# Linear attention behind a sparse feed-forward layer: gathers issued right behind GpSimd's buffer sums, and the query mean placed later in a batch's first tile

## The reference

```
xn  = layernorm(x)
out = x + attention(xn) + ffn(xn)

attention: q, k, v = xn @ w.T, 16 heads of 16; sq = elu(q) + 1; sk = elu(k) + 1
  memory: a_m = sq @ M_m, n_m = sq . z_m           (4 fine memories, and their sum as the coarse one)
          rel_m = mean over the 1024 tokens of n_m  -> w = softmax over the 4 memories
          out_fine = sum_m w_m * a_m / n_m ;  out_coarse = a / n
          e = sigmoid(relu(out_coarse @ w1 + b1) @ w2 + b2); mix of fine and coarse by e
  local : causal linear attention in chunks (scores = sq sk^T * mask, plus the carried state)
  output: per-head gate of memory and local, then @ w_o.T
ffn: 8 experts, top 2 of them for each token, and a shared expert
```

## Time and profile before

| | |
|---|---|
| median of 3 runs | 770.82 us (770.18 to 779.68) |
| the profiled execution's own time | 772.72 us |
| its span | 770.6 us |
| attention phase in the trace | about 360 to 771 us, 411 us |
| PE / DVE / ACT / POOL busy in 360 to 771 us | 352.0 / 286.3 / 208.2 / 209.5 us |
| one steady batch, from the start of tile (2,0) to that of (3,0) | about 99 us |

### The profile page before, as it was taken

How to read it: one execution, slowest core, us unless ns; L and a number is a source line. 1 busy time by engine, 2 the same in 40 slices (tenths; PEclk the granted TensorE clock), 3 DMA queues, 4 the chain that set the end, 5 groups by cost and what they waited for, 6 DMA issues and landing times.

```text
span 770.6 us, 23124 instructions
## 1 busy us (share of the span) xinstructions
PE 659.8 (86%) x8226; PEld 546.0 (71%) x8226; DVE 511.3 (66%) x1362; ACT 362.8 (47%) x902; POOL 310.0 (40%) x406
## 2 busy tenths in 40 slices
PE   1988888795999999997799998989988899889892
PEld 1776767583999999996577676776766767667671
DVE  3756565385666666666387577875778766777772
ACT  4544444343444444444454655544545546464441
POOL 1172727165810000002146554554554636546653
PEclk9998999897999999998899999999999999999995
DMA  8136363533533333334201112210222102011100
GB/s 265 54 130 210 126 215 125 188 114 134 161 123 110 120 119 114 121 119 133 94 3 30 46 55 83 71 30 20 80 73 81 31 16 84 16 52 52 59 24 28
DMA packets 60109, 71.42 MB, mean 93 GB/s; under 512 B 7596, under 2 KB 55052, under 8 KB 60012
## 3 DMA queue, kind: packets, MB, share of 16 engines
q1 hardware_dynamic: 50940, 52.61, 21.0%
q0 software_dynamic: 6656, 16.86, 6.6%
q10 hardware_dynamic: 2416, 0.59, 0.4%
HBM read 38.45 MB, written 31.59 MB: 91 GB/s over the span
## 4 chain that ended last, share of the span: by engine, by line
PE 30%; DVE 13%; issue 7%; ACT 2%; POOL 1%; DVEq 0%; POOLq 0%; ACTq 0%
PE a_ring L87 4%; PE a_sums L1457 3%; PE a_ring L1421 3%; PE a_ring L1443 3%; PE a_ring L89 3%; PE a_ring L88 3%; PE a_ring L1399 3%; PE a_ring L1368 2%; DVE probs L1636 2%; PE a_ring L1387 2%; PE a_ring L1432 2%; DVE mem_rows L1674 2%; PE a_ring L1409 1%; DVE rest L1658 1%; DVE mem_rows L1645 1%
## 5 line engine op out<-in xcount | busy, mean ns | idle before, releaser
L1718 POOL TENSOR_TENSOR mem_rows<-mem_rows 128x512 f32<-128x512 f32 x32 | 41.9, 1309 | 82.8 <-DVE mem_rows L1674 82.8
L1697 POOL DMA_INDIRECT yg<-d_grouped_y,from_row x64 | 62.4, 975 | 15.6 <-issue 11.7
L1694 POOL TENSOR_TENSOR tick_a<-lane 128x1 f32<-128x1 f32 x32 | 7.2, 224 | 145.6 <-POOLq L834 145.6
L1711 POOL TENSOR_TENSOR yg<-yg 128x256 f32<-128x256 f32 x32 | 26.2, 817 | 86.8 <-ACT yg L1519 86.7
L1503 ACT ACTIVATE with_mem<-a_ring 128x340 f32<-128x340 f32 x128 | 47.8, 460 | 17.8 <-PE a_ring L1368 11.4
L87 PE MATMUL e_up<-wb,xb 128*128 x144 | 53.0, 368 | 0.5 <-issue 0.5
L978 ACT ACTIVATE hb<-e_h 88x256 fp32r<-88x256 f32 x72 | 27.5, 382 | 52.3 <-PE e_h L953 52.3
L87 PE MATMUL e_y<-wd,hb 88*128 x146 | 48.8, 334 | 1.0 <-DVE hb L1017 1.0
L1010 DVE TENSOR_TENSOR h_sb<-e_up,silu 128x176 f32<-128x176 f32 x72 | 24.6, 342 | 35.4 <-ACT silu L973 35.4
L1636 DVE TENSOR_TENSOR probs<-a_ring,causal 128x256 f32<-128x256 f32 x128 | 45.0, 411 | 3.8 <-PE a_ring L1387 3.7
L89 PE MATMUL e_up<-wb,xb 128*128 x144 | 46.9, 326 | 0.0
(11 more groups left out here) (295 smaller groups left out, 2083.6 us busy)
## 6 DMA issues: line engine op xcount, KB each, us to landing
xg<-d_rows SPq DMA_DIRECT2D x77, 128.0 KB, 2.0
d_grouped_y<-y_sb SPq DMA_DIRECT2D x73, 128.0 KB, 1.8
d_base<-xn_in SPq DMA_DIRECT2D x8, 512.0 KB
xn_in<-d_xn SPq DMA_DIRECT2D x4, 1024.0 KB
total<-d_base SPq DMA_DIRECT2D x8, 512.0 KB, 4.5
out<-total SPq DMA_DIRECT2D x8, 512.0 KB, 3.1
mem_rows<-in_w_up SPq DMA_DIRECT2D x4, 704.0 KB
v<-in_x_tok SPq DMA_DIRECT2D x2, 1024.0 KB
```

Source lines behind the costliest of these rows:

```text
L1697: pool.indirect_dma_start(yg[tile % GATHERS][:, k, :], None, d["grouped_y"], bass.IndirectOffsetOnAxis(ap=c["from"][:, k, tile:tile + 1], ...
L1718: link(pool.tensor_tensor(part[:, :, :, :], prod[:, :, 0:2, :], prod[:, :, 2:4, :], ALU.add))
```

## The change

Two edits. The step mean goes behind fold(b,0,0), ahead of the norms steps, instead of ahead of keys. And `fetch` is called at step outT, behind L1712 of the same tile, with a wait for that very add, instead of at the next tile's step fine behind L1722. The numbers of fetches and of all other instructions stay. Scores are still products of 64 columns against keys masked by parity, in both.

```diff
@@ -1115,12 +1115,12 @@
         order.append(("coarseT", b, t, 0))
         if not i:
             order += [("q", 1, 1, 0), ("q", 1, 1, 1)]
-        if t == 0:
-            order.append(("mean", b, 0, 0))
         order += [("keys", b, t, 0), more[0]]
         if i > 1:
             order.append(("oproj", *tiles[i - 2], 0))
         order += [("state", b, t, 0), ("hidden", b, t, 0), ("fold", b, t, 0)]
+        if t == 0:
+            order.append(("mean", b, 0, 0))
         if i + 1 < len(tiles):
             order += [("norms", *tiles[i + 1], j) for j in range(NB3)]
         if t == 0:
@@ -1711,6 +1711,9 @@
                         link(pool.tensor_tensor(rows[:, 0, :], rows[:, 0, :], rows[:, 1, :], ALU.add))
                         pool.tensor_tensor(total[:, t, :], total[:, t, :], rows[:, 0, :],
                                            ALU.add).then_inc(s_ysum, 1)
+                        if tile + GATHERS < B * NT:
+                            since(pool, s_ysum, b * NT + t + 1)
+                            fetch(tile + GATHERS)
                     elif what == "fine" and j == KC - 1:
 
                         since(pool, s_prod, b * KC * NT + KC * (t + 1))
@@ -1720,10 +1723,6 @@
                         link(pool.tensor_tensor(att[:, :].rearrange("p (g n) -> p g n", g=NP),
                                                 part[:, :, 0, :], part[:, :, 1, :], ALU.add))
                         pool.tensor_tensor(att[:, :], att[:, :], rest[:, :], ALU.add).then_inc(s_att, 1)
-                        tile = (b - 1) * NT + t
-                        if tile and tile - 1 + GATHERS < B * NT:
-                            since(pool, s_ysum, b * NT + t)
-                            fetch(tile - 1 + GATHERS)
 
```

## The result

| | before | after |
|---|---|---|
| median of 4 runs | 770.97 us | 748.35 us (744.26 to 752.97) |
| ratio of the runs | | 0.9685, 95% interval 0.9601 to 0.9769 |
| span of the profiled execution | 770.6 us | 742.4 us |
| start of attention (first L1340 on PE) | 360.3 us | 350.5 us |
| attention, from there to the end of PE's last product | 401.9 us | 383.5 us |

The change makes the kernel 3.1% faster; 1.5% had been forecast. Medians here are of all runs, while a ratio leaves out the runs that took over 1.5% longer than the fastest of their kernel. Of the 28.2 us between the two spans, 9.9 lie ahead of attention, where both kernels are the same.

The account below looks back on a forecast made before the run. No engine was taken to bound the kernel; the attention chain hops between PE, DVE and ACT. Gains of 9.1 + 2.8 less 0.2 made 11.7 us, forecasting a 759.1 us median, range 754 to 766.

Parts of the forecast that it names:

- The mean, first tiles: First tile of each batch: moving the mean behind fold saves 2.8 us in the first batch, 3.05 in each other.
- the ring: First tiles, batches 2 to 4: oproj takes the first score step's bank, so a 0.6 us wait replaces 1.87.
- DVE kept up: First tiles: PE's gain passes through DVE, with the elu product of k(b,1,1) 3.0 to 3.4 us earlier.
- the clock's share: First tiles, batches 2 to 4: the stall's low clock cost another 0.9 and 0.6 us, which the move wins back.
- no clock is to be won here: First batch's first tile: granted clock was 1.00 behind the stall, so the 2.8 us gain includes none from clock.
- by itself moving them earlier is worth nothing: Gathers moved earlier: no gain, since no wait of ACT for a gather is in the list of waits.
- Their cost on POOL: Moved gathers start POOL's fine sum 0.65 us later: some 0.15 us lost in one tile, taken as 0.2.
- Wait or clock stays: Rival, first tiles: the wait only moves or the clock falls anyway, costing 4.6 us; time 763.7, chance 0.24.
- the port rival: Rival: POOL's shifted sums change their meetings with DVE at the port; up to 5 us more gain, 754, chance 0.11.
- the half that was to give time: Meetings of DVE with POOL's sums at elu products and reciprocals go, giving up to 5 us more.
- others come: As POOL's three sums move by 0.65 us, some new meetings with DVE instructions arise; no separate size given.
- Stretched calls: Rival, L1697 between L1712 and L1718: calls of 1.9 us instead of 0.97 cost 15.7 us; 774.8, chance 0.05.

Follow-up runs that it names:

- E1: Only the mean moved, gathers left in place, against the kernel before on a chip where that takes 733 us: 718.52 us against 733.41, ratio 0.9807.
- E7: Only the mean moved, as a repeat on a chip where the kernel before takes 770 to 780 us: 776.48 us, ratio 1.0002 to it.
- E8: Only the gathers moved, mean in its old place, on a chip where the kernel before takes 770 to 780 us: 761.35 us, ratio 0.9884 to it.
- E4: The full change again, unedited, against the kernel before on the chip where that takes 733 us: 720.95 us, ratio 0.9852.
- E14: The full change a third time, on a chip where the kernel before takes 770 to 780 us: 760.73 us against 779.88, ratio 0.9824.
- E5: The kernel before, unedited, traced a second time on a chip where it takes 770 to 780 us: 774.11 us, beside a median of 779.67 there.
- E11: Mean moved, fetches in the old place, the loop's calls bringing 64 bytes a row instead of 1024: 766.36 us against 769.92, unclear as a ratio.
- E12: Mean moved, fetches in the old place, the loop's indirect DMAs replaced by plain ones from fixed rows: 746.86 us against 779.88 before, ratio 0.9638.
- E13: Mean moved, fetches in the old place, one indirect call per fetch in the loop instead of two: 751.48 us, ratio 0.9701 to the kernel before.

## Why the prediction was wrong

**The mean, first tiles: right in mechanism, the size partly by luck.** Forecast 2.8 and three times 3.05; the iterations lost 2.2, 3.2, 3.3 and 3.3 us. The wait moved to oproj as rebuilt from the ring (0.47 us instead of 0.6), DVE kept up (the elu product L1584 of k(b,1,1) at 464.07, 9.6 us behind coarseT; before it was 12.3), and the clock's share came back with the idle. But that share is not the same in each execution, and I had one trace. In the six traces with the mean in its old place coarseT to norms takes 6.6 us in five first tiles of batches 2 to 4 (the clock stays high), 8.2 in eleven and 9.7 in two, behind the same 1.87 us of idle; with the mean moved it is 5.4 in all 30, of ten traces. The first batch's tile took 17.3 to 17.5 us in three of them and 22.0 to 22.5 in the other three, against 14.5 to 15.9 with the mean moved: "no clock is to be won here" was true of the trace that I had. That is a likely part of the 14.9 us of E1. One part was missed: values move too, and I never asked what else runs at their new time. On the slow kind that alone takes back the gain of the three first tiles concerned (E7).

**The gathers: the step that failed is "by itself moving them earlier is worth nothing".** I priced the calls by who waits for them and what they hold up on POOL. They have a third price, which they put on PE on the slow kind of chip: when indirect calls run beside PE's 64-column products, PE pauses for 0.4 us at a time, up to three times a fetch, and in half of the cases the clock falls behind that. The trace of before had shown it: the iterations (2,4) and (3,4) were 3.6 us longer than they are without, and their rows carry "issue" three times in a row. I had read such rows as part of the tile. By E8 the moved gathers give 8.6 us on that kind of chip where I had a loss of 0.2.

**Their cost on POOL: the term was too small, and half of the path was missing.** The fine sum is 2.66 us behind the base sum in the row above, 0.65 later, as forecast. On the fast kind the cost was 2.4 us (E4 against E1), where I had 0.2 in one tile: outT waits for att in (4,4), (4,5) and (4,6), 0.3, 1.3 and 1.3 us, and DVE meets POOL's last sum in each first tile. On the slow kind outT waits for att no more than before (5.5 us, twice, in both traces), and the second price alone is seen.

**The rivals.** "Wait or clock stays" is what the mean alone does on the slow kind, for a reason that it didn't name. Of the port rival, the half that was to give time is in no run; "others come" is L1624 above, some 1 us in three batches. Stretched calls: the longest of all traces took 1.49 us, all others 0.94 to 1.25, never 1.75. So no trace shows a call held up for a whole product of DVE, let alone all of them; a call of 1.25 us does stand behind the wait of (4,6) in E4.

**The size.** On the fast kind 12.5 us were measured for 11.7, and that agreement is in part luck: the mean gave 14.9 for 11.9, and the gathers took 2.4 for 0.2. On the slow kind attention gave 18.4 us by trace, and 17.3 for E14 against E5; the medians gave 22.6 and 19.2. Of the 10.8 us by which the first median lies under the forecast, 6.7 are attention's surplus; the other 4.1 lie within the scatter ahead of it. How the phases ahead of attention fall accounts for up to 11 us between two executions.

**What stays open.** Not shown is what in an indirect call stops PE. It isn't the bytes (E11), nor a transfer as such on that queue, nor the number of its packets (E12): in (1,4) of the kernel before the first pause begins at 425.78, and the calls' first packet starts at 426.60. With one call there are fewer pauses (E13). A fetch of PE's instructions that the calls hold up would fit, but no run tests it, and the packets that the profile counts as instruction are in flight in only 24 of the 109 pauses of over 0.3 us in the traces of before, E5, E7 and E11. Another open rival is the reading of the row numbers, which the plain DMAs don't do. Nor is it shown why one chip is free of it; as each chip was used at one time only, chip and time aren't told apart either.

## What to carry to other kernels

Price a moved instruction three ways: who waits for it, what it holds up on its engine, and what the other engines are doing at its new time, above all runs of small products; do the same for everything that your edit makes earlier. "Issue" waits that repeat inside a run of equal products are a finding and not noise: look for what runs on GpSimd beside them. A single one ahead of a run can be a wait under a wrong name: compare it with the same place in another trace. Read what a stall costs in clock from more than one trace. Compare two edits alone and together, and on more than one chip, before you credit either.

## What the runs showed of the hardware

- Indirect DMA calls of GpSimd beside PE's 64-column products: PE pauses of 0.34 to 0.45 us at L1421 (0.30 to 0.48 at L1387), mostly five or six products apart, beginning while a call runs or up to 0.3 us behind its end, in the kernel before and in each kernel with fetches left in the old place on the slow kind of chip; none in the four traces on the fast chip. Plain DMAs of the same bytes from the same queue: none (E12).
- Behind three such pauses the granted clock fell in six of twelve iterations t = 4 (before, E5, E7, E11), with products of 512 columns 0.43 us apart instead of 0.24. Those six took 16.2 to 17.8 us, the other six 14.7 to 14.8, against 12.6 without pauses.
- The same 1.87 us of idle ahead of the mean left the granted clock high in five first tiles of 18 and let it fall for part of the stretch in 13.
- The same kernel took 733 us on one chip and 770 to 780 on others; attention of the changed kernel 373.0 against 383.5 us.
- In the changed kernel on the slow kind, an idle of 0.5 to 0.7 us ahead of L1421 in (2,1) and seven more iterations is called "issue". L1421 starts 0.26 us behind the end of DVE's L1682 in all of them, as it does on the fast chip, where such an idle is put down to DVE: it is that wait. Inside the runs of the changed kernel pauses of at most 0.32 us are left.
